# Queries stacked ahead of upper keys, a second batch's projections ahead, and fp32r halves for the third attention's scores, in a four-layer transformer kernel

## The reference, cut to what matters

```
x = x + attention_0(norm(x), ctx, mask)      16 heads of 16, biases
x = x + experts_0(norm(x))
x = x + attention_1(norm(x), ctx)            1 head of 256
x = x + experts_1(norm(x))
x = x + attention_2(norm(x), ctx)            16 heads of 64
x = x + experts_2(norm(x))
x = x + attention_3(norm(x), ctx, mask)      16 heads of 16, no biases
x = x + dense_3(norm(x)), then a last layer norm
```

```
q = (x @ Wq.T) in heads of 64;  k = (ctx @ Wk.T);  v = (ctx @ Wv.T)
sim = q @ k.T * 0.125;  attn = softmax(sim);  out = (attn @ v) @ Wo.T + bo
```

## Time and profile before

| | us |
|---|---|
| median of 3 runs (2401.43 to 2405.17) | 2403.71 |
| the profiled execution | 2400.26 |
| span of its records | 2398.4 |
| TensorE busy in the span | 2236.1 (93%) |
| VectorE busy | 1186.2 (49%) |
| ScalarE busy | 1044.0 (44%) |

### The profile page before, as it was taken

How to read it: one execution, slowest core, us unless ns; L and a number is a source line. 1 busy time by engine, 2 the same in 40 slices (tenths; PEclk the granted TensorE clock), 3 DMA queues, 4 the chain that set the end, 5 groups by cost and what they waited for, 6 DMA issues and landing times.

```text
span 2398.4 us, 44743 instructions
## 1 busy us (share of the span) xinstructions
PE 2236.1 (93%) x15310; PEld 1711.2 (71%) x15310; DVE 1186.2 (49%) x3453; ACT 1044.0 (44%) x2859; POOL 350.8 (15%) x393
## 2 busy tenths in 40 slices
PE   5999998999988899999999999999869979999998
PEld 4777877677766667777777777777647757777765
DVE  4777774222245522454554554554542256777613
ACT  3777773222223222244444444444312257778711
POOL 2000001111144255100000000000024310000020
PEclk8999998999999899999999999999979989999999
DMA  7666666222255322200000000010232177766400
GB/s 187 188 173 160 172 152 250 77 83 87 84 149 183 121 71 65 63 21 8 19 26 15 11 18 8 11 53 1 92 127 66 61 209 183 182 161 167 102 12 23
DMA packets 152698, 230.52 MB, mean 96 GB/s; under 512 B 66368, under 2 KB 127120, under 8 KB 149920
## 3 DMA queue, kind: packets, MB, share of 16 engines
q1 hardware_dynamic: 139808, 195.30, 28.5%
q0 software_dynamic: 10656, 29.37, 3.7%
q10 hardware_dynamic: 2016, 3.00, 0.5%
HBM read 176.36 MB, written 51.25 MB: 95 GB/s over the span
## 4 chain that ended last, share of the span: by engine, by line
PE 83%; DVE 7%; issue 3%; DMA 3%; ACT 1%; SPq 1%; POOL 1%; ACTq 0%; DVEq 0%; POOLq 0%
PE bank L1068 10%; PE bank L1859 9%; PE bank L1099 7%; PE bank L1892 6%; PE bank L979 6%; PE bank L975 6%; PE bank L1924 5%; PE bank L1005 4%; PE bank L1056 4%; PE bank L990 3%; PE bank L1051 3%; PE bank L964 3%; PE bank L1909 3%; PE bank L986 3%; PE bank L2208 2%
## 5 line engine op out<-in xcount | busy, mean ns | idle before, releaser
L1068 PE MATMUL bank<-ident,arena 112*125 112x112 f32 x2352 | 374.1, 277 | 4.6 <-ACT arena L1334 0.5
L1068 PEld LDWEIGHTS bank<-ident,arena 112*125 112x125 f32 x2352 | 336.2, 188 | 53.1 <-issue 13.1
L1327 ACT ACTIVATE arena<-arena,mx 112x375 f32<-112x375 f32 x512 | 309.5, 605 | 117.0 <-DVE mx L1273 114.6
L1273 DVE CUSTOM_DVE_ANT_0 arena<-bank,maskf 112x375 f32<-112x375 f32 x512 | 271.3, 541 | 125.9 <-PE bank L1051 124.6
L1051 PE MATMUL bank<-kS,qS 128*112 128x376 f32 x512 | 233.2, 456 | 33.6 <-DMA qS<-query_halves 24.1
L1327 ACT ACTIVATE arena<-bank,mx 112x375 f32<-112x375 f32 x272 | 156.1, 576 | 186.5 <-DVE mx L1285 155.4
L1285 DVE TENSOR_REDUCE mx<-bank 112x1 f32<-112x375 f32 x256 | 128.9, 543 | 211.8 <-PE bank L1056 211.7
L1859 PE MATMUL bank<-arena 128*128 x532 | 229.5, 554 | 2.7 <-ACT arena L1985 1.4
L1294 DVE COPY arena<-bank 125x336 f32<-125x336 f32 x448 | 214.2, 502 | 33.5 <-PE bank L1068 33.5
L1099 PEld LDWEIGHTS bank<-arena 125*32 125x32 f32 (+1 forms) x4608 | 144.5, 119 | 85.9 <-issue 68.5
L1099 PE MATMUL bank<-arena 125*32 125x112 f32 (+1 forms) x4608 | 202.6, 265 | 3.0 <-DVE arena L1294 2.9
(11 more groups left out here) (243 smaller groups left out, 3416.4 us busy)
## 6 DMA issues: line engine op xcount, KB each, us to landing
kS<-key_halves SPq DMA_DIRECT2D x256, 188.0 KB, 3.8
key_halves<-arena SPq DMA_DIRECT2D x64, 376.0 KB, 4.1
arena<-in_ctxT SPq DMA_DIRECT2D x63, 376.0 KB, 4.5
arena<-in_f_out SPq DMA_DIRECT2D x21, 768.0 KB, 4.6
qS<-query_halves SPq DMA_DIRECT2D x256, 56.0 KB, 2.2
arena<-in_f_up SPq DMA_DIRECT2D x4, 2816.0 KB
arena<-results SPq DMA_DIRECT2D x38, 224.0 KB, 4.4
query_halves<-arena SPq DMA_DIRECT2D x32, 224.0 KB, 2.8
```

Of the source, the lines that this page charges most:

```text
L1068: m = pe.transpose(bank[2 + g % 2][0:KT, k * S:(k + 1) * S], pr[:, g % t.NR, k * KT:(k + 1) * KT], ident[0:S, 0:S])
L1273: dve.tensor_tensor_reduce(sm[:, g % 2, :], bank[g % 2][0:S, 0:SK], maskf[:, :], -t.a["scale"], 3e38, ALU.add, ALU.min, mx[:, g % t.NR:g % ...
L1327: act.activation(pr[:, g % t.NR, :], src, ACT.Exp, bias=mx[:, g % t.NR:g % t.NR + 1], scale=-1.0, accum_out=row_sum(t, b)[:, h:h + 1]).the ...
```

## The change

There are four parts.

1. **First attention, order.** For batch 0 the queries are projected before the second half of the keys and are spilled and stacked ahead of it. Batch 1's keys and values are projected ahead of the first scores. Its keys are spilled before its queries. Loads are moved: context 0 to the head of ScalarE's queue, six loads of `x` and the router's weights from ScalarE's queue to SyncE's behind batch 0's stacking. VectorE zeroes `qS` (GpSimd did), and GpSimd zeroes the second half of the padded values later, behind the first layer norm.
2. **Fourth attention, order.** Batch 1's values and keys are projected ahead of the first scores; its context is loaded earlier, and its keys are spilled ahead of its queries. In batch 0 nothing changes in the order of spills.
3. **Third attention, scores.** Queries and keys are kept as halves: ScalarE writes the upper (line 1373's place, and now the queries too), VectorE the lower by a subtraction, and only then is the bank free. A pair of heads takes six fp32r matmuls of 64 rows, three for each head, in alternation between the row halves. The pair waits for the probabilities of both heads before it.
4. **Third attention, order.** The keys' halves have one buffer, so key tile `o` of the next batch may only be projected after scores `2o` and `2o+1` of this one. `turns_of_keys` lays keys and values in alternation over the whole batch for this. `("wh", 1)` stays behind the keys in the list.

```diff
@@ Att.steps @@
+        def turns_of_keys(w, q, k, v, out):
+            k = [(step, cost, w + 2 * step[3]) for step, cost, _ in k]
+            if not k:
+                return out
+            return (q + k[0:1] + v[0:1] + k[1:2] + v[1:2] + k[2:3] + v[2:3] + k[3:4] + out + k[4:5] + v[3:4] + k[5:6]
+                    + v[4:5] + k[6:7] + v[5:6] + k[7:8])
...
             elif self.L == 0:
-                ahead = k[:1] + first + last + [turn] + k[1:] + [lower[1], ("mask",), lower[2]] + q + [lower[0]] + v
+                ahead = k[:1] + first + last + [turn, lower[1]] + q + [lower[0]] + k[1:] + [lower[2], ("mask",)] + v + k2 + lower2 + v2
             else:
-                ahead = [("mask",)] + k + lower[1:] + v + first + last + [turn] + q + [lower[0]]
+                ahead = [("mask",)] + k + lower[1:] + v + v2 + k2 + first + last + lower2 + [turn] + q + [lower[0]]
...
         def values_done(t, b):
-            return t.g0 + t.gen_index("v", b, NKT - 1, t.VH - 1) + 1
+            return t.g0 + max(t.gen_index("k", b, t.NO - 1), t.gen_index("v", b, NKT - 1, t.VH - 1)) + 1
...
@@ att_tensor, scores @@
-                    elif h == 0:
-                        freed_all(pe, t, "q", b)
-                        freed_all(pe, t, "k", b)
+                    elif t.halves:
+                        if h == 0:
+                            freed_all(pe, t, "q", b)
+                        freed(pe, t, t.gen_index("k", b, h // 2))
                     if g >= 2:
-                        pe.wait_ge(t.maxed if t.masked else t.probs, t.h0 + g - 1)
+                        pe.wait_ge(t.maxed if t.masked else t.probs, t.h0 + g - 1 + t.halves)
...
-                        rows = slice(h % 2 * dh, (h % 2 + 1) * dh)
-                        m = pe.matmul(bank[g % 2][0:S, 0:SK], qmv(t, b)[rows, h // 2, :], kTv(t, b)[rows, h // 2, :],
-                                      start=True, stop=True)
+                        for n, (qh, kh) in enumerate(((0, 0), (0, 1), (1, 0))):
+                            for j in range(2):
+                                rows = slice(j * dh, (j + 1) * dh)
+                                m = pe.matmul(bank[j][0:S, 0:SKE], qH[rows, b % 2, qh, h // 2, :], kH[rows, kh, h // 2, :],
+                                              start=(n == 0), stop=(n == 2))
+                                if n == 2:
+                                    m.then_inc(t.scores, 1)
+                        continue
...
@@ att_vector @@
+            if L == 0:
+                dve.memset(qS[:, :, :], 0.0)
...
+                if t.halves and kind in "qk":
+                    dve.wait_ge(t.upper, t.u0 + t.upper_of[(kind, b, o, h)])
+                    if kind == "q":
+                        ins = dve.scalar_tensor_tensor(out=qH[:, b % 2, 1, o:o + t.QG, :],
+                                                       in0=src[:, 0:t.QG * S].rearrange("p (o t) -> p o t", t=S),
+                                                       scalar=qscale, in1=qH[:, b % 2, 0, o:o + t.QG, :].bitcast(F32),
+                                                       op0=ALU.mult, op1=ALU.subtract)
+                    else:
+                        ins = dve.tensor_tensor(kH[:, 1, o, :], src[:, 0:SKE], kH[:, 0, o, :].bitcast(F32), ALU.subtract)
+                    ins.then_inc(t.gen_free[n % t.GB], 1)
+                    return
...
@@ att_scalar @@
+                if kind in "qk" and t.halves:
+                    if kind == "q":
+                        ins = act.activation(qH[:, b % 2, 0, o:o + t.QG, :],
+                                             src[:, 0:t.QG * S].rearrange("p (o t) -> p o t", t=S), ACT.Copy,
+                                             scale=-t.a["scale"])
+                    else:
+                        ins = act.activation(kH[:, 0, o, :], src[:, 0:SKE], ACT.Copy)
+                    ins.then_inc(t.upper, 1)
+                    return
...
@@ stack_sync @@
+                if b == 0 and t.L == 0:
+                    spill_keys(0)
+                    spill_queries()
+                    stack_keys(0)
+                    stack_queries()
+                    spill_keys(1)
+                    stack_keys(1)
+                    return
+                if b == 1:
+                    spill_keys(0)
+                    spill_keys(1)
+                    spill_queries()
+                    stack_keys(0)
+                    stack_queries()
+                    stack_keys(1)
+                    return
...
                 batch(b)
+                if b == 0 and t.L == 0:
+                    for pair in range(2, B // 2):
+                        rows_of_x(sp, pair)
+                    sp.dma_start(wR[:, :, :], A["f0_r"]).then_inc(loaded["r0"], 16)
                 if b == 0 and t.L:
-                    context(sp, t, 1)
                     for pair in range(1, 4):
                         results_back(sp, t, pair)
...
@@ the engines' programs @@
-            sp.dma_start(biasA[:, 1, :], A["a0_bk"]).then_inc(loaded["bias0"], 16)
             rows_of_x(sp, 0)
             weight_0(sp, 1, "k")
-            context(sp, att[0], 0)
+            sp.dma_start(biasA[:, 1, :], A["a0_bk"]).then_inc(loaded["bias0"], 16)
...
             context(sp, att[3], 0)
+            context(sp, att[3], 1)
...
-            pool.memset(part(V_AT, 2 * VPAD, KT), 0.0).then_inc(padded, 1)
-            pool.memset(qS[:, :, :], 0.0).then_inc(padded, 1)
+            pool.memset(part(V_AT, VPAD, KT), 0.0).then_inc(padded, 1)
...
         def _(act):
+            context(act, att[0], 0)
...
-            for pair in range(2, B // 2):
-                rows_of_x(act, pair)
-            act.dma_start(wR[:, :, :], A["f0_r"]).then_inc(loaded["r0"], 16)
```

56 lines of the change are left out of this document (37 added, 19 removed).

## The result

The changed kernel took 2409.66 us in the median of 20 runs (2404.22 to 2417.19), the kernel before beside it 2402.53 (20 runs, 2398.39 to 2406.67). The ratio is 1.0031 with an interval of [1.0022, 1.0040]: 0.3% slower, where 2385 us and faster was forecast. The profiled execution of the change took 2405.34 us.

A forecast was written before the change was run, and what follows sets the result against it. TensorE's work and idle times were taken to bound the kernel. Terms -11.6 - 5.1 - 15 + 3.9 + 8.7 = -19.1 took the profiled 2400.26 to 2381.2; with 3.4 for the median, 2385 us was forecast, range 2367 to 2402.

The forecast's parts named there:

- Part 1: First attention: earlier spills and stacking bring first scores and batches 1 and 2 sooner; -11.6 us, bounds -4 and -16.
- Part 2: Fourth attention: projections moved into idle time shorten batch 0 and bring batch 2 sooner; -5.1 us, bounds -2 and -9.
- Part 3, the pair of scores: Third attention: six fp32r matmuls side by side take 0.70 us a pair, not 0.82; -15 us for 128 pairs.
- Part 3, waits behind a key tile: Third attention: a value tile closely behind a key tile waits 0.85 us, not 0.30, seven times; +3.9 us.
- Part 4: Start of the third attention: values wait for weights split behind eight subtractions, then slower clock; +8.7 us, bounds +6 and +11.
- Part 3, "VectorE then works 27 of 45 us; the work that hides this is TensorE's": Third attention: VectorE's eight added subtractions a batch, 4.3 us, are hidden behind TensorE's work, except behind some key tiles.
- Rival C: Third attention: a subtraction ahead of the next maxima delays probabilities; 1 us a batch, +16, 2401 us; 9% chance.
- A batch longer than 45.3 us in the mean is C: Sign in the third attention: a mean batch time above 45.3 us would show Rival C.
- rival A: Third attention scores: row halves don't run side by side in fp32r, a pair takes 1.23 us; +48, 2452 us; 8% chance.

The follow-up runs named there:

- e1: The change with the third attention left as before, so only the starts of the first and fourth attention changed: 2387.39 us, 0.9932 of the kernel before.
- e11: The change with the three fp32r score products of one row half written in a row, then the other's three: 2416.99 us, 1.0056 of the kernel before.
- e8: The change with key tiles' lower halves subtracted for the first batch only, 120 subtractions taken away: 2388.06 us, 0.9932 of the kernel before.
- e9: The change with the layer norm's small steps ahead of their slot's key tile in VectorE's list: 2393.52 us, 0.9958 of the kernel before.
- e6: The change with the reciprocal of a finished batch's sums and its copy ahead of both query subtractions: 2405.98 us, 1.0014 of the kernel before.
- e12: The change with layer norm steps first, third attention's first values behind its first queries, and reciprocal between the query subtractions: 2373.69 us, 0.9874 of the kernel before.
- e13: The change with the reciprocal of a finished batch's sums and its copy between the two query subtractions: 2407.29 us, 1.0012 of the kernel before.
- e3: The change's order of key and value tiles, but third attention scores in float32 and evacuated as before, without subtractions: 2394.79 us, 0.9962 of the kernel before.

## Why the prediction was wrong

- *Part 1, -11.6.* Right in its sum and in its beginning: -12.1 at the last batch, queries spilled at 13.21, first scores 26.6 for 26.3. In between it was luck in part. Batch 0 took 19.3 us for the forecast 17.1 (the eight issues for batch 1's `qS` ended at 43.7, not 41.5), batch 2 came 10.4 us sooner for the forecast 11.6, and the last 1.7 us were gained behind it, for which the sum has no term.
- *Part 2, -5.1.* Right within its bounds: from the fourth attention's first scores to those of its last batch pass 309.5 us (311.5 in e1) for 316.1 before.
- *Part 3, the pair of scores, -15.* Right: 0.70 us for 0.82. e11 adds that this doesn't hang on their being written in turns.
- *Part 3, waits behind a key tile, +3.9.* Right: the seven waits ahead of value tiles rose from 2.1 to 5.4 us, 0.8 each (the 4.6 above are six of them, since one stands ahead of 1060 us).
- *Part 4, +8.7.* Right: +8.8 between the first and the third attention's first scores (a pause of 4.71 for the forecast 5.1, and 2.35 us lost to the slower values behind it for 1.7).
- *Part 3, "VectorE then works 27 of 45 us; the work that hides this is TensorE's".* This step failed: it put the eight subtractions at nothing but the 3.9. I compared VectorE's sum, 27 of 45 us, with TensorE's, and looked for lost cover only where the bank is handed on. But each subtraction makes VectorE wait in the middle of its list (161.1 us at the 128 of keys) for ScalarE's half, and so for a TensorE tile of the same slot. What stands behind it, `xn` behind a key tile and `on` behind the queries, inherits that wait, and TensorE wants those two at once. They cost 13.2 + 11.9 us for 1.1 before, 24 us. e8 and e9 show it from two sides for `xn`, and e6, e12 and e13 for `on`. With this term the stretch adds up: 120 pairs of scores give -14.4, `xn` +13.2, `on` +10.8, value tiles +3.3, query tiles +0.6, the low clock about +2: +15.5, where 685.1 - 669.3 = 15.8 were measured and -11 forecast.
- *The order in turns* was costed at nothing but the 3.9 too. Of e3's 7 us 5.0 are waits that the change doesn't have; the 2.7 us at `xn` that e3, e8, e9 and e12 still show are what is left for the order, and they are part of the 13.2.

Rival C was near in its price (+16, 2401) and wrong in its mechanism: I had put the cost on maxima and probabilities, and gave it 9%. "A batch longer than 45.3 us in the mean is C" was the right sign to look for: the mean is 685.1 / 15 = 45.7. But 45.3 was misread: it is 680 / 15, and the 680 us hold a little more than 15 batches. By the first scores of the batches, one took 669.3 / 15 = 44.6 us before, so the loss is 1.1 us a batch. A sum of rival A is wrong too. With a pair of 0.97 us its +19 stands in place of the -15, and the other terms are -4.1, so the whole would be +15; the sum turns at a pair of 0.85 us. Nothing hung on it, since the pair took 0.70.

## What to carry to other kernels

Where engines run through one list strictly in order, the question for an added step isn't whether its engine has time but what it waits for and what stands behind it: put steps that have all they need ahead of one that waits for a tile of the same slot. Don't mend it by letting the waiting step slip, if it frees one of two banks. And a change that comes out slower may hold a faster kernel: here three changes of order, without one instruction less, turned +7 us into -29.

## What the runs showed of the hardware

- Behind 22 of 49 pauses of TensorE of 1.9 us, in seven traces, the clock fell to 1.2 GHz, mostly for 3.4 us, at the most for 13.7. In e13 a pause of 1.89 us was followed by 7 us mostly at 1.2 GHz (granted clock 0.57 and 0.50), which cost 3.1 us more than the pause. In the seven traces whose pauses there were 0.9 us or shorter it never fell; in e9, with 0.4 us at the same place, the mean stayed at 1.00 over 620 us.
- Matmuls of 64 rows in the two row halves run side by side in fp32r as in float32 (0.82 us for four float32 instructions), and six of them take 0.70 to 0.71 us whether written in alternation or three and three. That the second half's matmuls start early although the first half's stand ahead of them was not expected.
